# Four of sixteen row-sum additions of a graph kernel moved from VectorE to adding transfers on GpSimd's queue

## The reference

```python
def L0(h, adj, W_neigh, b_neigh, W_self, b_self):
    deg = jnp.sum(adj, axis=1, keepdims=True) + 1e-05
    h_neigh = (adj / deg) @ h
    return relu(h_neigh @ W_neigh.T + b_neigh + h @ W_self.T + b_self)

def L1(x, adj, W, b):
    rowsum = adj.sum(axis=1)
    d = jnp.where(rowsum > 0, rowsum ** (-0.5), 0.0)
    return relu((d[:, None] * adj * d[None, :] @ x) @ W + b)

x = layernorm(x + L0(x, adj, ...))
x = layernorm(x + L1(x, adj, ...))
```

## Time and profile before

| | |
|---|---|
| time, median of 3 runs | 788.96 us (788.67 to 789.18) |
| the profiled execution: its own time | 789.72 us |
| its span, first to last instruction | 787.9 us |
| TensorE busy | 777.3 us (99%) |
| VectorE busy | 597.2 us (76%) |
| ScalarE busy | 397.1 us (50%) |
| GpSimd busy | 0.4 us (0%) |
| chain of work that ended last | TensorE 95%, DMA 2%, VectorE 2% |
| moved by DMA | 160.93 MB, 204 GB/s over the span |

### The profile page before, as it was taken

The page is one execution under the profiler, slowest core; times in us unless marked ns, Lnnn a source line. Parts: engine busy times, 40 slices in busy tenths (PEclk is TensorE's granted clock), DMA queues, the critical chain, the costliest instruction groups (busy, mean ns, idle before and its releaser), DMA issues.

```text
span 787.9 us, 11197 instructions
## 1 busy us (share of the span) xinstructions
PE 777.3 (99%) x3733; PEld 648.0 (82%) x3733; DVE 597.2 (76%) x919; ACT 397.1 (50%) x550; POOL 0.4 (0%) x7
## 2 busy tenths in 40 slices
PE   8999999999999999999999999999999999999996
PEld 5878888888888888888888888888888888888886
DVE  6999989989899899998976565565646546564554
ACT  4654644646446365454554545354453544544452
POOL 0000000000000000000000000000000000000000
PEclk9999999999999999999999999999999999999999
DMA  7965564755647557474575656656574665757551
GB/s 281 354 239 192 197 237 151 242 185 185 241 150 249 184 169 260 135 264 168 178 255 173 211 191 203 218 201 235 171 245 154 207 219 192 234 177 241 169 168 46
DMA packets 54316, 160.93 MB, mean 204 GB/s; under 512 B 5009, under 2 KB 18449, under 8 KB 54289
## 3 DMA queue, kind: packets, MB, share of 16 engines
q1 hardware_dynamic: 45936, 151.54, 56.4%
q10 hardware_dynamic: 8352, 9.05, 3.4%
HBM read 152.17 MB, written 8.39 MB: 204 GB/s over the span
## 4 chain that ended last, share of the span: by engine, by line
PE 95%; DMA 2%; DVE 2%; ACT 0%; issue 0%; SPq 0%
PE ps_main L797 83%; PE ps_epi L722 6%; PE ps_epi L710 2%; PE ps_main L819 1%; PE ps_main L780 1%; PE ps_epi L713 1%; DMA xt_sb<-xt 1%; DMA raw<-adj_t 1%; DMA acc<-x_nat 1%; DVE lo L450 1%; DVE acc L634 0%; PE ps_epi L744 0%; DVE xs L450 0%; PE ps_epi L829 0%; ACT hi L285 0%
## 5 line engine op out<-in xcount | busy, mean ns | idle before, releaser
L285 ACT ACTIVATE hi<-raw 128x1024 fp32r<-128x1024 f32 x254 | 268.8, 1059 | 255.0 <-PE ps_main L797 243.1
L450 DVE TENSOR_TENSOR lo<-raw,hi 128x1024 fp32r<-128x1024 f32 x254 | 309.9, 1220 | 98.9 <-ACT hi L285 98.4
L797 PE MATMUL ps_main<-hi,xs 128*128 128x512 f32 x1120 | 354.4, 391 | 1.4 <-DVE lo L450 1.4
L797 PE MATMUL ps_main<-hi,zs 128*128 128x512 f32 x880 | 275.2, 389 | 0.0
L797 PEld LDWEIGHTS ps_main<-hi,xs 128*128 128x128 f32 x1120 | 210.4, 188 | 45.7 <-issue 2.7
L797 PE MATMUL ps_main<-lo,xs 128*128 128x512 f32 x560 | 218.3, 390 | 0.0
L797 PEld LDWEIGHTS ps_main<-hi,zs 128*128 128x128 f32 x880 | 165.2, 188 | 33.8
L797 PE MATMUL ps_main<-lo,zs 128*128 128x512 f32 x440 | 171.2, 389 | 0.0
L634 DVE TENSOR_TENSOR acc<-acc,raw 128x1024 f32<-128x1024 f32 x112 | 136.1, 1215 | 0.0
L797 PEld LDWEIGHTS ps_main<-lo,xs 128*128 128x128 f32 x560 | 105.3, 188 | 20.6 <-issue 0.2
L797 PEld LDWEIGHTS ps_main<-lo,zs 128*128 128x128 f32 x440 | 82.6, 188 | 16.6
(11 more groups left out here) (102 smaller groups left out, 385.8 us busy)
## 6 DMA issues: line engine op xcount, KB each, us to landing
raw<-adj_t SPq DMA_DIRECT2D x256, 512.0 KB, 3.3
res<-x_nat SPq DMA_DIRECT2D x11, 512.0 KB, 6.3
xt_sb<-xt SPq DMA_DIRECT2D x8, 512.0 KB, 5.9
x_scratch<-tt ACTq DMA_DIRECT2D x8, 512.0 KB, 4.3
res<-x_scratch SPq DMA_DIRECT2D x8, 512.0 KB, 6.4
out<-tt ACTq DMA_DIRECT2D x7, 512.0 KB, 6.7
tt<-x_nat SPq DMA_DIRECT2D x3, 512.0 KB, 7.0
acc<-x_nat ACTq DMA_DIRECT2D x1, 512.0 KB, 5.0
```

The source lines that it names most:

```text
L285: return act.activation(dst, src, ACT.Copy)
L450: return dve.tensor_tensor(dst, src, hi_part.bitcast(f32), ALU.subtract)
L797: last = pe.matmul(ps[:, f, :], stationary(layer, part, jt, f), mov[:, slot(u), cols], start=(jt == 0 and i == 0), stop=(jt == JT - 1 and ...
```

## The change

Units 6, 8, 10 and 12 of each block in the first layer (`BY_DMA`) are no longer added by VectorE. GpSimd's queue loads the first of them from DRAM once more, into the half of `acc` that the block doesn't use, and lets three further transfers add the others onto it on the way, each after the one before has landed. It begins when the row sums of the block before are taken (`rs_summed`), in block 0 after the fourth `lo` (unit 5). At the end of the block VectorE waits for the fourth transfer, adds the two halves (a new instruction of 128x1024) and then folds. The loads of units 10, 12, 14 and, for the next block, 0 no longer wait for an addition. All matmuls, splits and raw loads stay as they are.

```diff
+BY_DMA = (6, 8, 10, 12)
...
+        dma_summed, acc_merged = sem("dma_summed"), sem("acc_merged")
...
-                        if layer == 0 or (is_first(b) and u < RING):
+                        if (layer == 0 or (is_first(b) and u < RING)) and (u - RING) % NU not in BY_DMA:
                             sp.wait_ge(acc_done, g0 + (u - RING + 1))
...
+            def sum_units(b, parity):
+                spare = acc[:, 1 - parity, :]
+                if is_first(b):
+                    pool.wait_ge(unit_done, WHOLE)
+                    wait_x_split(pool, 0)
+                    pool.wait_ge(l_ready, BY_DMA[0])
+                else:
+                    pool.wait_ge(rs_summed, b)
+                for i, u in enumerate(BY_DMA):
+                    if i == 0:
+                        pool.dma_start(spare, adj_in[b, u]).then_inc(dma_summed, 16)
+                    else:
+                        pool.wait_ge(dma_summed, (b * len(BY_DMA) + i) * 16)
+                        pool.dma_start(spare, adj_in[b, u], accum_op=ALU.add).then_inc(dma_summed, 16)
+
+            sum_units(0, 0)
+            with pool.Fori(1, NB - 1, 2) as b:
+                sum_units(b, 1)
+                sum_units(b + 1, 0)
+            sum_units(NB - 1, 1)
...
-                        if u > 1:
+                        if u > 1 and u not in BY_DMA:
                             dve.wait_ge(acc_done, g0 + u)
-                            dve.tensor_tensor(a, a, raw[:, slot(u), :], ALU.add).then_inc(acc_done, 1)
+                            dve.tensor_tensor(a, a, raw[:, slot(u), :], ALU.add)\
+                               .then_inc(acc_done, 2 if u + 1 in BY_DMA else 1)
                     place(u, 2)
                     if layer == 0 and u == NU - 1:
                         dve.wait_ge(acc_done, g0 + NU)
+                        dve.wait_ge(dma_summed, (b + 1) * len(BY_DMA) * 16)
+                        dve.tensor_tensor(a, a, acc[:, 1 - parity, :], ALU.add).then_inc(acc_merged, 1)
+                        dve.wait_ge(acc_merged, b + 1)
                         dve.tensor_tensor(a[:, 0:IB], a[:, 0:IB], a[:, IB:UW], ALU.add).then_inc(acc_folded, 1)
```

## The result

| | before | changed |
|---|---|---|
| median | 789.12 us (8 runs) | 791.69 us (8 runs, 790.48 to 792.11) |
| ratio to before, 95% interval | | 1.0027 (1.0018 to 1.0036) |
| profiled execution, span | 789.72, 787.9 us | 792.11, 790.0 us |

What follows compares the result with a forecast made beforehand. TensorE was taken as the bound, idle only 1.43 us before unit 12 in block 0. Terms -1.1 + 0 + 4.0 + 0 = +2.9 us on the median 788.96 gave 791.9 us; range 787.3 to 799.0.

Steps and rivals of the forecast that it cites:

- detailed signs: Block 0: xt's flight from 6.1 to 9 or 10 us, TensorE's wait before unit 12 from 1.43 to 4 to 5 us.
- The bound and the place: TensorE bounds the kernel; its only wait after the weight splits is 1.43 us before unit 12 in block 0.
- Term 1: Block 0: of 32 removed adds only that of unit 6 is on the chain, -1.1 us.
- Term 3: Block 0: GpSimd's transfers take DMA time before xt lands, delaying xt and unit 12, +4.0 us.
- the first of the three cases: Block 0: GpSimd's transfers wait behind what was issued before; two land before xt, taking 2.6 or 4.0 us.
- half and half: Block 0: both queues share the engines equally; 4.6 us per transfer at plain price, 4.6 to 4.8 us taken in all.
- Terms for the merge and the steady blocks: Eight merges have 4.9 us of cover for 1.22 us; steady blocks' transfers fit the half-empty stretch; 0 each.
- The chain as the bound: Rival, steady blocks: four serial transfers over 10.2 us each stall TensorE, +24 us at 11 us each; chance 0.08.
- VectorE's busy time: Whole run: falls from 597.2 to about 568 us with 32 adds removed and 8 merges added.

## Why the prediction was right

The total was right (791.9 forecast, 791.69 measured), and so were its sign and place. The mechanism was right too: the transfers' time on the DMA engines delays `xt`, and the delay is kept. That the two numbers agree within 0.2 us is luck: the flight of `xt` alone scattered by more. The detailed signs came short of what was named: a flight of 8.26 us where 9 to 10 were expected, waits of 3.41 us where 4 to 5 were.

- **The bound and the place.** Right. The whole loss is the later start of unit 12 in block 0: 2.14 us of a span that grew by 2.1. Blocks 1 to 7 alone measured 0.9997.
- **Terms 1 and 3 together.** The prediction has `xt` land 4.0 - 1.1 = 2.9 us later; it landed 2.15 us later (38.10 against 35.95).
- **Term 1, -1.1 us for the add of unit 6.** Its size is right: 0.9980 without any transfer, and in the run with the late start `xt` was issued at 28.96. In the profile after, it can't be seen at the issue of `xt` (29.84 against 29.87). The prediction followed VectorE's list and left the other thing that this issue waits for, the landing of the weights, at its old time. Those loads share the DMA engines with GpSimd's first transfer and came 1.27 us later (ScalarE waited 2.3 us for the first of them, 2.4 with the adds kept, and about 1.0 in every profile that started late without a transfer ahead). That swallowed the 1.1, and with the add put back the issue was at 29.80. In the execution of block 0 alone that started early, the weights were in time and VectorE was the link again (27.89), so the weights don't hold `xt` in every execution. The text also overlooked that in the kernel before VectorE's own list was nearly as long as the path over `xt`.
- **Term 3, +4.0 us for the transfers.** The price was about right, 1.53 and 3.18 us against 1.32 and 2.64. Two transfers counted, as the first of the three cases had it; the third was issued at 37.89, 0.2 us before `xt` landed. What failed is that both were put on the landing of `xt` whole. The copy had landed at 27.85, 2 us before `xt` was issued; what it took can only have held up earlier loads, the weights among them. Only the second, issued at 28.16, flew beside `xt`, whose flight is 2.18 us longer (8.26 less 6.08; 2.27 with the adds kept). Laid against the runs without the adds, all the transfers of block 0 cost 3.5 to 3.8 us, near the 4.0; how the loss divides between the two terms depends on what it is laid against.
- **What stays open.** Without a newcomer ahead the flight of `xt` was 4.2, 4.3, 4.63, 4.80, 6.08 and 6.29 us in six profiles; with newcomers it was 8.26 to 9.00 in four (7.61 with plain copies). What makes the first group so wide was not tried, so 2.18 us is one pair and not the price of a transfer.
- **How the two queues share.** The cases were: behind what was issued before (6 to 7 us), or half and half (4.6 us). GpSimd's first transfer, issued at 21.25, landed after 6.6 us, where the load of ws issued 1.1 us before it took 8.3; the second, issued at 28.16, needed 9.4 where `xt` took 8.26. That speaks for the first case, though not for a strict line: it landed 0.6 us before ws. DMA: Bandwidth & Descriptors in the Trainium skill (Queues, rings and completion order) has the engines take packets in turn from the queues. I had read that as half and half, and by it had written 792.5 for the total. The trace does not agree with this reading: by my estimate of 4.6 us, a transfer that had half of the engines would have landed near 25.9, and it landed near 27.9.
- **Terms for the merge and the steady blocks, 0.** Right. The merge's cover held (the fold follows it at 203.00), and more than it needed: the DMA share in the steady stretch rose by 0.38, not by the 0.2 that I had spread over the whole block, and still no raw block came late enough for TensorE. ScalarE's longer wait for raw blocks (29.6 us) ended before anyone needed it.
- **The chain as the bound.** Rightly given little, but it was nearer than the prediction has it. In block 0 I expected the fourth transfer before 50. It was issued at 47.77 and flew 7.2 us, to 55.0, and VectorE came to the merge at 55.34: 0.3 us to spare. The run with the late start shows the price beyond that point, over 14 us in one block, 3.1 of them for the lower clock after the wait.
- **VectorE's busy time**: 573.9 us against the 568 forecast. Neighbouring instructions overlap by 0.08 us and the busy time counts that once, so a removed add gives back 1.14 us, not 1.22; that accounts for (32 - 8) x 0.08 = 1.9 of the 5.9 us, and the rest was not traced.

## What to carry to other kernels

Work moved from a busy engine to the DMA queues paid here only where that engine is on the chain, and it was charged to the transfers on the chain (first the weights, then `xt`). Both were the same 16 us of the first block: the freed VectorE was worth 1.3 us there, the borrowed DMA time cost more, and everywhere else neither mattered. Before timing such a change, look which load is the next link, put the new transfers behind it, and check that a serial chain of them still ends before its consumer; or take the one add off the chain by order, which gave as much for nothing.

## What the runs showed of the hardware

- A transfer that adds on the way takes 3.18 us of all 16 DMA engines for 512 KB, a plain one from the same queue 1.53 us. From issue to landing GpSimd's transfers take 5.4 us in the median of all 32, where the loads of raw blocks before took 3.3 us in the median, and an adding one holds GpSimd itself for 0.86 us.
- The DMA engines are one pool. In the full stretch (20.4 to 36 us) the DMA share went from 0.99 to 1.03 and the rate stayed at 363 GB/s: the newcomers' bytes came out of the others'. The Trainium skill says the same (DMA: Bandwidth & Descriptors, Issuing engines are not separate DMA queues), and this case agrees with it.
- TensorE starts in two ways; three of the eleven profiles started early. In the profile of before the first 16 matmuls on loaded data take 9.02 us and the split units begin at 14.29; in that of the run without transfers they take 7.13 us and the split units begin at 12.19 (timeline of TensorE, before and then that run):

```profile
5.84 9.02 PE L780 MATMUL ps_main<-raw,acc 128*128 128x512 f32 x16 [1.02 <-DMA acc<-x_nat]
```

```profile
5.62 7.13 PE L799 MATMUL ps_main<-raw,acc 128*128 128x512 f32 x16 [0.80 <-DMA acc<-x_nat]
```

The granted clock is given as 1.00 from 8 to 14 us in both. The times of some kernels fall into two groups, with block 0 alone 789.0 to 790.1 and 791.3 to 792.2. An early start was seen in three profiled executions: 786.31 us without transfers, the shortest of its eleven, 790.11 us of block 0 alone, in the shorter group, and 790.89 us with two transfers, the fourth shortest of its nine. That the start makes the groups was not tried. It is why positions of two profiles were compared only where both started alike; of the run with two transfers only the flight and the waits were used.
